# Second graph layer of a fused graph network kernel: weights multiplied first, edge matrix in six blocks, new order at the head

## Chip, cores and metric

The kernel runs on one core of one Trainium2 chip. The metric is the device time of one execution in microseconds, the median of several runs. All times of the trace are counted from the first instruction of the profiled execution.

## What is computed

Two layers on 1250 nodes with 512 features. Each layer adds a graph part and an attention part to x, and then an expert part. The change touches the graph part of the second layer. The reference, cut to it (N = 1250 here, D = 512):

```python
exp_e = jnp.exp(weighting_gate - m)
row_sum = jax.ops.segment_sum(exp_e, src, num_segments=n_nodes)
atten_e = exp_e / (row_sum[src] + 1e-06)
Mfeat = source_features @ Wm + bm                       # 1250 x 256
out0 = jax.ops.segment_sum(atten_e[:, None] * Mfeat[dst], src, num_segments=n_nodes)
out1 = jax.ops.segment_sum(atten_e[:, None] * Mfeat[src], dst, num_segments=n_nodes)
h = jnp.concatenate([out0, out1], axis=-1) @ W1 + b1    # 512 -> 128
h = jax.nn.relu(_layernorm(h, gamma, beta))
h = jax.nn.relu(h @ W2 + b2)                            # 128 -> 512
return jnp.where((row_sum > 0)[:, None], h, 0.0)
```

The sum of this, of x and of the attention part goes through a layer norm, is routed to two banks of eight experts, and the experts' outputs are added.

## The kernel before

Everything runs in one program. Each engine has its own instruction stream, written out by hand, and semaphores order the streams. Nodes are cut into 10 tiles of 125 rows (`NT`, `TP`) and into three column groups of 500, 500 and 250 (`CH`), which hold tiles 0 to 3, 4 to 7 and 8 to 9 (`GROUPS`).

**The order of TensorE's work** is the list `MIX` (line 119 and on). Job j writes bank j mod 8 of PSUM; `begin` (L602) waits until the job eight places earlier has been evacuated; `mx_full` counts finished jobs. VectorE (DVE) and ScalarE (ACT) wait for jobs by name with `mx_wait`.

**Precision.** Ordinary products are split: a float32 operand is stored as a high part and a low part of type float32r, and three products are added (`rows_job`, lines 620 to 622, and `cols_job`, lines 631 to 633). The neighbour sums use plain float32 operands; each of their matmuls stands as two MATMUL records with a weight load each in the trace.

**The edge matrix** (1250 x 1250, the sum of exp(edge weight) over the edges of each pair of nodes) was built at the start and lies in DRAM as `d_w` and transposed as `d_wt`. In the second layer it is read back in slabs of one column group each: `load_slab(i)` (L1234), i = 0 to 2 from `d_wt`, 3 to 5 from `d_w`. There are three homes in SBUF (`slab_home`, L382), so slab i + 3 takes the home of slab i. All six are issued from ACT's DMA queue: 0 after the copies of `bf`, 1 and 2 after the last copy of `x`, 3 to 5 inside the loop at L1320, each after its home's last reader.

**The stretch that is changed, on TensorE:**

- attention jobs `v`, `bq`, `bk`, `source`, `sink` (L816, L826, L832). Between them the features `g`: 10 tiles, xn @ Wm with 256 columns, split precision. ACT copies them to `MfA` (L1254).
- `back`, `bf`, `kv` (L912), `x` (L919) and then `p`, the attention's output projection (10 tiles, 12 matmuls of 512 columns each).
- `rinv` (L930): the inverse row sums turned into rows of 128 equal partitions.
- `ma` and `mb` (L939), 6 jobs each, one for each column group and each half m of the 256 features: 10 matmuls with 128 feature columns as weights and a slab of 500 or 250 columns streamed. DVE scales `ma` by `rinv` into `V` (L1949); ACT and DVE split both into `XH` and `XL`.
- `w1` (`head_in`, L953): 10 tiles, 12 matmuls of 128 columns, the product with W1.
- per group: `head_row` (L1961: add b1, statistics), `spreads` and `scales` (mean, inverse deviation), `head_norm`, ACT's `head_relu` (L1332), `th` (transposes, L964), ACT's `head_cols` (L1337), DVE's `head_low` (L1981), `hd` (`head_out`, L972 to L975: product with W2, four matmuls a tile), ACT's relu (L1359), DVE's `add_row` and statistics of the final layer norm, `norm_rows` (L1111), `store_rows` (L1353), transposes `t7` (L613), `to_cols` (L1084), `low_cols` (L1456), router logits `lg` (L1000 to L1004), `lgt` (L1011).

POOL splits each weight unit into its two parts (L2936, L2938); a unit is 2048 columns. The unit `g1` holds Wm, W1 and W2. The same unit is loaded again as `g1b` for W1 and W2. SP loads the expert weights (`load_bank`, L2851) once the jobs `mb` 5 and `th` 2 are done. ACT's order at the head, as it stands before:

```python
head_cols(0); root(6, 1); head_relu(1); root(6, 2); head_rows(0); head_relu(2)
head_cols(1); head_cols(2); head_rows(1, 2, 3, 4, 5); root(7, 0) ...
```

Of the kernel before, what the change touches and what calls it, by code (L numbers as in the profile page):

```python
# [17 lines left out]
N = 1250  # L18
# [47 lines left out]
COLS = {"bq": 0, "mb1": 4, "fb1": 6, "bs1": 6 + 2 * E0}  # L66
NCOL = 8 + 2 * E0
# [35 lines left out]
def all_of(name, k):  # L103
# [36 lines left out]
       + [("bk", m) for m in range(4)] + [("v", 9), ("shift", 1)]  # L140
# [32 lines left out]
def program(nc, A, out):  # L173
    ctx = ExitStack()
    with ctx:
# [138 lines left out]
        MfA = A3[0:TP, :].rearrange("p (t d) -> p t d", t=NT)  # L314
        MfB = R1[0:TP, 0:NT * 256].rearrange("p (t d) -> p t d", t=NT)
        hg = A3[0:TP, 0:NT * 128].rearrange("p (t d) -> p t d", t=NT)
# [65 lines left out]
        slab_home = [at(AT_Q, NT * 500), A1[:, 0:NT * 500], A2[:, 0:NT * 500]]  # L382

        def slab_of(i):
            return slab_home[i][0:TP, :].rearrange("p (t e) -> p t e", t=NT)
# [49 lines left out]
        slab_loaded = [sem(f"slab_loaded{i}") for i in range(3)]  # L435
# [85 lines left out]
        heavy_rounded = sem("heavy_rounded")  # L521
# [23 lines left out]
        msg_high = sem("msg_high")  # L545
        msg_low = sem("msg_low")
# [28 lines left out]

        def rows_normed(eng, site, t):
            eng.wait_ge(normed_rows, NT * (site - (site > 1)) + t)
# [21 lines left out]
        def stream_pe(pe, n, unit, unit_done):  # L599
# [130 lines left out]
            pe.wait_ge(heavy_ready, 1)  # L730
# [135 lines left out]
            for i in range(3):  # L866
                pe.wait_ge(lo_ready, i + 1)
                for m in range(4):
                    spread_job("bq", 0, 4 * i + m)
                rows_gemm(("v", 6 + i), 6 + i, Hv, Lv, D)  # L870
            for m in range(4):
                spread_job("bk", 1, m)
# [54 lines left out]
            for i, (c0, w) in enumerate(CH):  # L927
                o = begin(("rinv", i))
                for t in range(c0 // TP, (c0 + w) // TP):
                    last = pe.matmul(o[:, TP * t - c0:TP * t - c0 + TP],  # L930
                                     lhsT=rinv[0:TP, t:t + 1].to_broadcast([TP, 128]),
                                     rhs=ident[0:TP, 0:TP], start=True, stop=True, skip_group_check=True)
                last.then_inc(mx_full, 1)

            def message_feature(name, src, i, m):
                c0, w = CH[i]
                o = begin((name, 2 * i + m))[:, 0:w]
                for t in range(NT):
                    last = pe.matmul(o, lhsT=src[:, t, 128 * m:128 * m + 128], rhs=slab_of(i)[:, t, 0:w], start=t == 0,  # L939
                                     stop=t == NT - 1, skip_group_check=True)  # L940
                last.then_inc(mx_full, 1)

            for i in range(3):
                pe.wait_ge(slab_loaded[i], 16)
                pe.wait_ge(features_ready, 1)
                for m in range(2):
                    message_feature("ma", MfA, i, m)
            pe.wait_ge(features_ready, 2)
            Hw, Lw = unit()
            Hw1, Lw1 = (x[:, 1024:1536].rearrange("p (k n) -> p k n", k=KC) for x in (Hw, Lw))  # L950
            Hw2, Lw2 = (x[:, 1536:2048].rearrange("p (k n) -> p k n", k=1) for x in (Hw, Lw))

            def head_in(g):  # L953
                pe.wait_ge(msg_low, 6)
                for m in range(2):
                    mx_evacuated(pe, ("mb", 2 * g + m))
                for t in GROUPS[g]:
                    rows_job(("w1", t), XH, XL, t, Hw1, Lw1, KC, 128)

            def head_turn(g):  # L960
                o = begin(("th", g))
                for t in GROUPS[g]:
                    pe.wait_ge(hg_ready, t + 1 + (g > 1))
# [14 lines left out]
            for i in range(3):  # L978
                pe.wait_ge(slab_loaded[i], 32)
                for m in range(2):  # L980
                    message_feature("mb", MfB, i, m)
                if i:
                    head_in(i - 1)
            head_turn(0)
            head_in(2)
            head_out(0)
            head_turn(1)
            head_turn(2)
            head_out(1)
            turn_group("t7", 7, 0, lambda t: R1t[:, t, :])  # L990
            head_out(2)
            unit_done()

            for g, (c0, w) in enumerate(CH):
                if g < 2:
                    turn_group("t7", 7, g + 1, lambda t: R1t[:, t, :])
# [2245 lines left out]
```

## Time and profile before

| | |
|---|---|
| runs | 1695.72, 1695.84, 1699.32 us; median 1695.84 us |
| span of the profiled execution | 1690.6 us |
| median less span | 5.2 us |
| TensorE busy | 1555.0 us, 92% of the span, 8983 matmul records |
| weight loads busy | 1214.2 us |
| DVE, ACT, POOL busy | 989.6, 445.7, 305.1 us |
| mean granted TensorE clock | 0.972 of full speed |

The execution of the profile has a span, from its first to its last instruction; the time of a run counts some microseconds more around it. A busy TensorE is not a TensorE at its peak, since matmuls are pipelined; the start to start distance of its records tells what one costs.

### The profile page before, as it was taken

To read this page: it belongs to the slowest core of one execution; us is meant where nothing else is said; L and a number is where in the kernel's file an instruction comes from. 1 tells how busy PE (TensorE), PEld (TensorE's weight loads), DVE (VectorE), ACT (ScalarE), POOL (GpSimd) and SP (SyncE) were. 2 spreads that over 40 slices of the span, in tenths; PEclk is the share of its full clock that TensorE was granted. 3 is DMA by queue.
4 is the path that set the end of the run, shared out by engine and by line. 5 is a ranking of instruction groups with operands and counts; after the bars stand their busy time and mean duration, and the time that the engine had idled before them with its cause. 6 is when DMAs were issued, how large, how long until landed. Compare 5 with 4: busy or idle time off the path is not lost.

```text
span 1690.6 us, 23793 instructions
## 1 busy us (share of the span) xinstructions
PE 1555.0 (92%) x8983; PEld 1214.2 (72%) x8983; DVE 989.6 (59%) x1767; ACT 445.7 (26%) x854; POOL 305.1 (18%) x191
## 2 busy tenths in 40 slices
PE   4798988897999999999998999998999999898998
PEld 3686877776777777877786788877757755676765
DVE  7878767889954672397256666665154511763332
ACT  4423111223311220130124242434215101441222
POOL 1000002053111031004001222212211000004565
PEclk9899998999999999999998999999999999899999
DMA  5122324341230020011001010100101322529343
GB/s 158 45 71 91 105 88 164 118 146 52 88 114 27 1 69 25 1 50 68 25 1 51 25 50 26 50 25 26 51 14 53 115 86 80 206 71 316 55 80 44
DMA packets 52138, 123.93 MB, mean 73 GB/s; under 512 B 8417, under 2 KB 28792, under 8 KB 44894
## 3 DMA queue, kind: packets, MB, share of 16 engines
q1 hardware_dynamic: 14026, 65.34, 11.3%
q10 hardware_dynamic: 28147, 46.81, 8.0%
q0 software_dynamic: 9856, 10.28, 3.5%
q8 instruction: 74, 1.21, 0.3%
q14 instruction: 35, 0.29, 0.0%
HBM read 92.87 MB, written 40.22 MB: 79 GB/s over the span
## 4 chain that ended last, share of the span: by engine, by line
PE 75%; DVE 11%; DMA 5%; issue 3%; ACT 3%; POOL 1%; PEld 0%; DVEq 0%; ACTq 0%; PEldq 0%; SPq 0%; POOLq 0%
PE ps L620 9%; PE ps L621 9%; PE ps L622 9%; PE ps L2288 6%; PE ps L678 4%; PE ps L680 4%; PE ps L631 4%; PE ps L632 4%; PE ps L633 4%; PE ps L939 3%; PE ps L3045 3%; PE ps L3067 3%; PE ps L826 2%; DMA d_w<-arena 2%; DMA arena<-d_w 2%
## 5 line engine op out<-in xcount | busy, mean ns | idle before, releaser
L620 PE MATMUL ps<-wslot,XH 128*125 128x512 f32 (+2 forms) x560 | 214.9, 384 | 5.4 <-DVE XL L1456 3.9
L621 PE MATMUL ps<-wslot,XH 128*125 128x512 f32 (+2 forms) x560 | 212.9, 380 | 0.0
L622 PE MATMUL ps<-wslot,XL 128*125 128x512 f32 (+2 forms) x560 | 212.6, 380 | 0.0
L2936 POOL CAST wslot<-arena 128x2048 fp32r<-128x2048 f32 x25 | 47.7, 1908 | 798.3 <-PEq L3013 428.5
L631 PE MATMUL ps<-XH,wslot 128*128 128x500 f32 (+1 forms) x336 | 123.2, 367 | 17.6 <-DVE XL L1456 10.6
L1461 DVE TENSOR_TENSOR arena<-ps,arena 125x512 f32<-125x512 f32 x150 | 98.2, 684 | 51.3 <-PE ps L622 45.3
L620 PEld LDWEIGHTS ps<-wslot,XH 128*125 128x125 f32 x560 | 104.8, 187 | 31.3 <-issue 4.4
L678 PE MATMUL ps<-CTr,Hhi 125*128 125x500 f32 (+1 forms) x360 | 125.0, 361 | 0.0
L632 PE MATMUL ps<-XH,wslot 128*128 128x500 f32 (+1 forms) x336 | 121.8, 362 | 0.0
L633 PE MATMUL ps<-XL,wslot 128*128 128x500 f32 (+1 forms) x336 | 120.9, 360 | 0.0
L622 PEld LDWEIGHTS ps<-wslot,XL 128*125 128x125 f32 x560 | 104.6, 187 | 22.7
L621 PEld LDWEIGHTS ps<-wslot,XH 128*125 128x125 f32 x560 | 104.7, 187 | 21.9 <-issue 0.2
L2288 PE MATMUL ps<-arena 125*128 x1330 | 96.0, 228 | 26.1 <-DVE arena L2562 22.3
L2938 POOL TENSOR_TENSOR wslot<-arena,wslot 128x2048 fp32r<-128x2048 f32 x25 | 117.1, 4685 | 2.0
L680 PE MATMUL ps<-CTr,Hlo_head 125*128 125x500 f32 (+1 forms) x324 | 109.8, 352 | 0.0
L2288 PEld LDWEIGHTS ps<-arena 125*128 125x128 bf16 x1330 | 83.2, 102 | 33.6 <-issue 33.4
L2562 DVE TENSOR_SCALAR arena<-arena 125x1280 bf16<-125x1280 int16 x133 | 73.0, 573 | 43.6 <-PE ps L2288 42.8
L631 PEld LDWEIGHTS ps<-XH,wslot 128*128 128x128 f32 x336 | 65.6, 195 | 31.9 <-issue 18.7
L939 PE MATMUL ps<-arena 125*128 125x500 f32 (+1 forms) x240 | 84.6, 513 | 1.4 <-DMA arena<-d_w 1.4
L1510 DVE TENSOR_TENSOR V<-ps,BC 128x500 f32<-128x500 f32 (+1 forms) x36 | 21.3, 592 | 107.3 <-PE ps L684 106.6
L678 PEld LDWEIGHTS ps<-CTr,Hhi 125*128 125x128 f32 x360 | 67.8, 188 | 15.1 <-issue 5.6
L1129 ACT ACTIVATE V<-V,cols 128x500 f32<-128x500 f32 (+1 forms) x96 | 56.0, 631 | 85.1 <-DVE V L1764 85.1
(445 smaller groups left out, 3074.7 us busy)
## 6 DMA issues: line engine op xcount, KB each, us to landing
arena<-in_units SPq DMA_DIRECT2D x29, 1024.0 KB, 4.8
arena<-in_units SPq DMA_DIRECT2D x8, 2048.0 KB, 11.8
d_w<-arena ACTq DMA_DIRECT2D x10, 625.0 KB
d_wt<-arena ACTq DMA_DIRECT2D x10, 625.0 KB, 4.1
rows<-in_rows ACTq DMA_DIRECT2D x22, 256.0 KB, 4.0
d_kv<-V SPq DMA_DIRECT2D x20, 250.0 KB
arena<-d_kv SPq DMA_DIRECT2D x20, 250.0 KB
arena<-d_wt ACTq DMA_DIRECT2D x2, 2441.4 KB
```

The source lines that it names most:

```text
L620: pe.matmul(o, lhsT=xh[:, k, s], rhs=H4[:, k, 0:nw], start=k == 0, stop=False, skip_group_check=True)
L621: pe.matmul(o, lhsT=xh[:, k, s], rhs=L4[:, k, 0:nw], start=False, stop=False, skip_group_check=True)
L622: last = pe.matmul(o, lhsT=xl[:, k, s], rhs=H4[:, k, 0:nw], start=False, stop=k == K - 1, skip_group_check=True)
L631: pe.matmul(o, lhsT=H4[:, k, f], rhs=XH[:, k, c0:c0 + w], start=k == 0, stop=False, skip_group_check=True)
L632: pe.matmul(o, lhsT=L4[:, k, f], rhs=XH[:, k, c0:c0 + w], start=False, stop=False, skip_group_check=True)
L633: last = pe.matmul(o, lhsT=H4[:, k, f], rhs=XL[:, k, c0:c0 + w], start=False, stop=k == KC - 1, skip_group_check=True)
L678: pe.matmul(o, lhsT=Hhi[0:TP, t, f], rhs=CTr[0:TP, t, c0:c0 + w], start=t == 0, stop=False, skip_group_check=True)
L680: pe.matmul(o, lhsT=Hlo[t][0:TP, f], rhs=CTr[0:TP, t, c0:c0 + w], start=False, stop=False, skip_group_check=True)
L939: last = pe.matmul(o, lhsT=src[:, t, 128 * m:128 * m + 128], rhs=slab_of(i)[:, t, 0:w], start=t == 0, stop=t == NT - 1, skip_group_check=True)
L1461: dve.tensor_tensor(dst, o[0:TP, 0:D], other, ALU.add).then_inc(mx_sem(name), 1)
L2288: last = pe.matmul(ps[:, 3 * (b % 2) + t // 4, 128 * (t % 4):128 * (t % 4) + 128], lhsT=buffer[:, 128 * t:128 * t + 128], rhs=pre_flat[:, ...
L2938: pool.tensor_tensor(wL[unit_slot(u)], wraw, wH[unit_slot(u)].bitcast(F32), ALU.subtract).then_inc(w_ready, 1)
```

## The change

1. The program computes Wm @ W1 on the chip. The unit `g1` now holds Wm transposed. Two new jobs `gw` (12 matmuls each, 256 columns, split precision) give a 512 x 256 matrix, one half for each half of W1; `gb` (4 float32 matmuls, 256 columns) gives bm @ W1. They stand between `v` 8 and `bk` 0. ACT copies them to SBUF, POOL splits the product into high and low part over the place of Wm in `g1`'s slot, and TensorE waits for that (`gw_step` 3) before the jobs `g`. The jobs `g` keep their shape and now give the features times W1, 2 x 128 columns (`GF`).
2. The jobs `rinv`, `ma`, `mb` and `w1` go. In their place are ten jobs `m`, one a tile: 20 float32 matmuls with 125 columns of a slab as weights and 128 columns of `GF` streamed. All copies, scalings and splits of the messages go; DVE's `head_row` scales the first half by `rinv` and adds the other and b1.
3. Each of the six slabs has a home of its own, each is loaded in two DMAs (partitions 0 to 111 and 112 to 124), the three of `d_w` from SP's queue and the three of `d_wt` from ACT's. Waits: after `bf`, after `kv`, after the last `x` (two), after the last `p` (two).
4. The head runs in a new order, and SP's bank loads wait for `m` 7 and `m` 9 instead. `hg` lies in `V`. Some semaphores are split or joined (`heavy_ready`, `hg_normed`, `hd_ready`, `norm_turn`). POOL's routing constants no longer wait for `ma`.

```diff
+       + all_of("gw", 2) + [("gb", 0)] + [("bk", m) for m in range(4)] + [("v", 9), ("shift", 1)]
...
-       + [("x", i) for i in range(12)] + [("p", t) for t in range(10)] + [("rinv", i) for i in range(3)]
-       + all_of("ma", 6) + all_of("mb", 4) + by_tile("w1")[0] + [("mb", 4), ("mb", 5)] + by_tile("w1")[1] + [("th", 0)]
-       + by_tile("w1")[2] + by_tile("hd")[0] + [("th", 1), ("th", 2)] + by_tile("hd")[1]
-       + turned("t7")[0] + by_tile("hd")[2] + turned("t7")[1] + [("lg", 0)] + turned("t7")[2] + [("lg", 1), ("lg", 2)]
+       + [("x", i) for i in range(12)] + [("p", t) for t in range(10)] + all_of("m", 8) + [("th", 0), ("m", 8)]
+       + by_tile("hd")[0] + [("th", 1), ("m", 9)] + by_tile("hd")[1] + turned("t7")[0] + [("th", 2), ("lg", 0)]
+       + by_tile("hd")[2] + turned("t7")[1] + [("lg", 1)] + turned("t7")[2] + [("lg", 2)]
...
+        slab_at = [(AT_Q, AT_R1), (AT_AR, AT_AR + NT * D), (AT_XX, AT_XX + NT * 250)]
...
+        def load_slab(eng, g, half):
+            c0, w = CH[g]
+            for a, b in ROW_PARTS:
+                eng.dma_start(slab_of(g, half)[a:b, :, :],
+                              d_wt[0:N, c0:c0 + w].rearrange("(t p) e -> p t e", p=TP)[a:b, :, :] if half == 0
+                              else d_w[:, a:b, c0:c0 + w].rearrange("t p e -> p t e"))\
+                   .then_inc(slab_loaded[g], 16)
...
+            pe.wait_ge(w_ready, n.unit + 2)
...
+            for i in range(2):
+                o = begin(("gw", i))
+                for c in range(2):
+                    oc = o[:, 256 * c:256 * c + 256].rearrange("p (s n) -> p s n", s=2)
+                    f = slice(256 * i + 128 * c, 256 * i + 128 * c + 128)
+                    for k in range(2):
+                        pe.matmul(oc, lhsT=Ht[:, k, f], rhs=Hw1[:, k, :, :], start=k == 0, stop=False, skip_group_check=True)
+                        pe.matmul(oc, lhsT=Ht[:, k, f], rhs=Lw1[:, k, :, :], start=False, stop=False, skip_group_check=True)
+                        last = pe.matmul(oc, lhsT=Lt[:, k, f], rhs=Hw1[:, k, :, :], start=False, stop=k == 1,
...
+            pe.wait_ge(gw_step, 3)
...
+            def message_rows(t):
+                g = min(t // 4, 2)
+                s = slice(TP * t - CH[g][0], TP * t - CH[g][0] + TP)
+                pe.wait_ge(slab_loaded[g], 64)
+                o = begin(("m", t))
+                for half, feature in enumerate((GA, GB)):
+                    for k in range(NT):
+                        last = pe.matmul(o[0:TP, 128 * half:128 * half + 128], lhsT=slab_of(g, half)[:, k, s],
+                                         rhs=feature[:, k, :], start=k == 0, stop=k == NT - 1, skip_group_check=True)
...
+            head_turn(0)
+            message_rows(8)
+            head_out(0)
+            head_turn(1)
+            message_rows(9)
+            head_out(1)
+            turn_group("t7", 7, 0, lambda t: R1t[:, t, :])
+            head_turn(2)
+            router(0)
+            head_out(2)
+            unit_done()
+            turn_group("t7", 7, 1, lambda t: R1t[:, t, :])
+            router(1)
+            turn_group("t7", 7, 2, lambda t: R1t[:, t, :])
+            router(2)
...
 # ACT
-            for t in range(3, NT):
+            for t in range(3, 9):
                 copy_v(t)
+            for i in range(2):
+                o = mx_wait(act, ("gw", i))
+                act.activation(gw_raw[:, 512 * i:512 * i + 512], o, ACT.Copy).then_inc(mx_sem(("gw", i)), 1)
...
-            load_slab(0)
+            load_slab(act, 0, 0)
...
+            load_slab(act, 1, 0)
+            mx_wait(act, ("p", NT - 1))
+            load_slab(act, 2, 0)
...
+            root(6, 1)
             head_cols(0)
             head_relu(1)
+            head_rows(0, 1, 2, 3)
+            head_cols(1)
+            root(7, 0)
+            norm_rows(7, 0)
+            store_rows(0)
             root(6, 2)
+            head_rows(4, 5)
             head_relu(2)
+            head_rows(6, 7)
+            to_cols("t7", GROUPS[0])
             head_cols(2)
             root(7, 1)
...
 # DVE
             def head_row(t):
+                o = mx_wait(dve, ("m", t))
+                own(dve.scalar_tensor_tensor(hg[:, t, :], o[0:TP, 0:128], rinv[0:TP, t:t + 1], row("gnnA", 128, 256), ALU.mult,
+                                             ALU.add))
+                settle()
+                dve.tensor_tensor(hg[:, t, :], o[0:TP, 128:256], hg[:, t, :], ALU.add).then_inc(mx_sem(("m", t)), 1)
...
+            head_row(8)
+            for t in range(3):
+                head_sum(t)
+            head_low(1)
+            head_sum(3)
+            spreads(0)
+            scales(7, 0)
+            head_row(9)
             spreads(2)
+            head_sum(4)
             scales(6, 2)
             head_norm(2)
+            for t in (5, 6, 7):
+                head_sum(t)
+            spreads(1)
+            low_cols(6, "t7", GROUPS[0])
+            head_low(2)
+            scales(7, 1)
...
 # SP and POOL
-            sp.wait_ge(mx_full, MJ[("mb", 5)] + 1)
+            sp.wait_ge(mx_full, MJ[("kv", 0)] + 1)
+            load_slab(sp, 0, 1)
+            mx_evacuated(sp, ("x", 11))
+            load_slab(sp, 1, 1)
+            sp.wait_ge(mx_full, MJ[("p", NT - 1)] + 1)
+            load_slab(sp, 2, 1)
+            sp.wait_ge(mx_full, MJ[("m", 7)] + 1)
             load_bank(0, 0)
             load_bank(0, 2)
-            sp.wait_ge(mx_full, MJ[("th", 2)] + 1)
+            sp.wait_ge(mx_full, MJ[("m", 9)] + 1)
             load_bank(0, 4)
...
+                if u == UNITS.index("g1"):
+                    pool.wait_ge(gw_step, 1)
+                    pool.tensor_copy(wH[unit_slot(u)][:, 0:1024], gw_raw).then_inc(gw_step, 1)
+                    pool.wait_ge(gw_step, 2)
+                    pool.tensor_tensor(wL[unit_slot(u)][:, 0:1024], gw_raw, wH[unit_slot(u)][:, 0:1024].bitcast(F32),
+                                       ALU.subtract).then_inc(gw_step, 1)
```

## Rows read from the trace of the kernel before

**Rows 1.** The page: span and busy time, share of each engine.
```profile
span 1690.6 us, 23793 instructions
PE 1555.0 (92%) x8983; PEld 1214.2 (72%) x8983; DVE 989.6 (59%) x1767; ACT 445.7 (26%) x854; POOL 305.1 (18%) x191
```

**Rows 2.** The chain that ended last, message stage: start, length, what.
```profile
1349.98 2.49 PE ps L930 x20
1352.47 33.55 PE ps L939 x80
...
1386.76 25.83 DMA arena<-d_w
```

**Rows 3.** Timeline of TensorE: start, length, line, operation, count, idle before.
```profile
1352.30 58.90 PE L939 MATMUL ps<-arena 125*128 125x500 f32 x160
1412.63 17.03 PE L939 MATMUL ps<-arena 125*128 125x500 f32 x40 [1.43 <-DMA arena<-d_w]
...
1448.38 0.61 PE L964 MATMUL ps<-ident,arena 125*128 125x125 f32 x4
...
1492.84 1.26 PE L1011 MATMUL ps<-ident,BC 16*125 16x16 f32 x10
```

**Rows 4.** Windows: stretch, length, busy PE, PEld, DVE, ACT, POOL, clock, DMA.
```profile
1434.70:1443.20 8.50, 8.50 (x40) 7.46 (x40) 1.00 0.00 0
...
1429.10:1434.70 5.60, 5.60 (x51) 5.37 (x49) 2.40 (x7) 1.87 (x2) 0.00 (x0) 1.00 0.00 0
...
1451.40:1492.80 41.40, 33.75 (x124) 18.92 (x123) 30.43 (x87) 23.44 (x44) 0.00 (x0) 0.79 0.58 208
```

**Rows 5.** L912's own records (min/median/max ns); windows of L912 and L3045, columns as rows 4.
```profile
L912 PEld LDWEIGHTS ps<-arena x80: 192/192/333, 1302.6 to 1312.1; 125*128 125x128 f32 x80
L912 PE MATMUL ps<-arena x80: 274/275/421, 1302.8 to 1312.2; 125*128 125x128 f32 x80
...
1302.80:1304.00 1.20, 1.18 (x6) 1.20 (x7) 0.50 0.89 370
...
1543.90:1545.70 1.80, 1.78 (x16) 1.59 (x15) 1.00 1.00 412
```

**Rows 6.** Windows of the feature jobs g 0 to 3 and 4 to 9; columns as rows 4.
```profile
1269.30:1275.20 5.90, 5.90 (x50) 5.77 (x50) 0.08 (x1) 1.62 (x4) 0.00 (x0) 1.00 0.01 3
...
1284.10:1292.90 8.80, 8.69 (x73) 8.49 (x73) 0.41 (x1) 2.50 (x7) 0.00 (x0) 1.00 0.00 0
```

**Rows 7.** Timeline of POOL, the splitting of g1 and of the unit behind it.
```profile
1211.03 4.63 POOL L2938 TENSOR_TENSOR wslot<-arena,wslot 128x2048 fp32r<-128x2048 f32 x1
1258.40 1.89 POOL L2936 CAST wslot<-arena 128x2048 fp32r<-128x2048 f32 x1 [42.74 <-PEq L3013]
```

**Rows 8.** Windows with slab loads, then with stores in two parts; columns as in rows 4.
```profile
1310.00:1320.00 10.00, 9.16 (x39) 5.44 (x38) 6.05 (x10) 2.93 (x5) 0.00 (x0) 1.00 0.33 128
...
1470.50:1479.00 8.50, 4.72 (x23) 3.34 (x23) 5.57 (x17) 4.34 (x9) 0.00 (x0) 0.90 0.76 247
```

**Rows 9.** Timeline of TensorE: tiles hd 1 and hd 2. Then ACT: norm of two rows.
```profile
1452.73 0.50 PE L972 MATMUL ps<-wslot,HH 128*125 128x512 f32 x1
...
1454.05 0.49 PE L972 MATMUL ps<-wslot,HH 128*125 128x512 f32 x1
...
1477.56 1.52 ACT L1111 ACTIVATE arena<-arena,small 125x512 f32<-125x512 f32 x2 [3.23 <-DVEq L1445]
```

**Rows 10.** Timeline of DVE: a norm pair, an add with its statistics, four low parts.
```profile
1438.46 0.35 DVE L1448 SCALAR_TENSOR_TENSOR arena<-arena,small,rows 125x128 f32<-125x128 f32 x1
...
1439.11 0.35 DVE L1448 SCALAR_TENSOR_TENSOR arena<-arena,small,rows 125x128 f32<-125x128 f32 x1
...
1460.44 0.69 DVE L1461 TENSOR_TENSOR arena<-ps,arena 125x512 f32<-125x512 f32 x1
1461.16 0.69 DVE L1419 BATCH_NORM_STATS2 small<-arena 125x6 f32<-125x512 f32 x1
...
1474.16 2.43 DVE L1456 TENSOR_TENSOR XL<-ps,XH 128x500 fp32r<-128x500 f32 x4
```

More of the change, by code:

```diff
@@ L432, in program @@
         ktot = V[0:TP, 0, :]
-        slab_loaded = [sem(f"slab_loaded{i}") for i in range(3)]
+        slab_loaded = [sem(f"slab_loaded{g}") for g in range(3)]
+        gw_step = sem("gw_step")
+        hg_normed = sem("hg_normed")
+        hd_ready = sem("hd_ready")
         ew_turned = sem("ew_turned")
@@ L870, in stream_pe @@
                 rows_gemm(("v", 6 + i), 6 + i, Hv, Lv, D)
+            pe.wait_ge(w_ready, n.unit + 2)
+            after = unit_slot(n.unit + 1)
+            H_, L_ = wH[after], wL[after]
+            Ht, Lt = (w[:, 0:1024].rearrange("p (k n) -> p k n", k=2) for w in (H_, L_))
+            Hw1, Lw1 = (w[:, 1024:1536].rearrange("p (s k n) -> p k s n", s=2, k=2) for w in (H_, L_))
+            for i in range(2):
[7 more added lines that the diff above has]
+                        last = pe.matmul(oc, lhsT=Lt[:, k, f], rhs=Hw1[:, k, :, :], start=False, stop=k == 1,
+                                         skip_group_check=True)
+                last.then_inc(mx_full, 1)
+            o = begin(("gb", 0))[0:TP, 0:256].rearrange("p (s n) -> p s n", s=2)
+            for k in range(2):
+                for part, w1 in enumerate((Hw1, Lw1)):
+                    last = pe.matmul(o, lhsT=cols[:, COLS["bm"] + k:COLS["bm"] + k + 1].to_broadcast([128, TP]),
+                                     rhs=w1[:, k, :, :].bitcast(F32), start=k == 0 and part == 0, stop=k == 1 and part == 1,
+                                     skip_group_check=True)
+            last.then_inc(mx_full, 1)
             for m in range(4):
@@ L926, in stream_pe @@
             unit_done()
[L927 to L932, printed above, removed]
-                last.then_inc(mx_full, 1)
[L935 to L947, printed above, removed]
+            def message_rows(t):
[7 more added lines that the diff above has]
+                                         rhs=feature[:, k, :], start=k == 0, stop=k == NT - 1, skip_group_check=True)
+                last.then_inc(mx_full, 1)
             pe.wait_ge(features_ready, 2)
+            for t in range(8):
+                message_rows(t)
             Hw, Lw = unit()
-            Hw1, Lw1 = (x[:, 1024:1536].rearrange("p (k n) -> p k n", k=KC) for x in (Hw, Lw))
             Hw2, Lw2 = (x[:, 1536:2048].rearrange("p (k n) -> p k n", k=1) for x in (Hw, Lw))
[L953 to L958, printed above, removed]
             def head_turn(g):
@@ L976, in head_out, with router @@
                               skip_group_check=True).then_inc(mx_full, 1)
[L978 to L996, printed above, removed]
+            def router(g):
+                c0, w = CH[g]
                 group_in_cols("t7", g)
@@ L1337, in head_cols @@
                 act.activation(HH[:, 0, c0:c0 + w], o[:, 0:w], ACT.Copy).then_inc(hg_high, 1)
[L1339 to L1340 removed]
             root(6, 0)
             head_relu(0)
[L1343 to L1344 removed]
+            row_ready(act, "gnnb2")
+            act.activation(HH[0:64, 1, 0:D], row("gnnb2")[0:64, :], ACT.Copy).then_inc(hg_high, 1)
             act.wait_ge(w_ready, len(UNITS))
             act.dma_start(b2e, A["b2e"]).then_inc(b2e_loaded, 16)
[L1347 to L1348 removed]
             def store_rows(g):
@@ L1386, in stream_act @@
             store_rows(2)
-            for g, (c0, w) in enumerate(CH):
-                o = mx_wait(act, ("lg", g))
-                act.activation(logits_R[:, c0:c0 + w], o[0:E1, 0:w], ACT.Copy).then_inc(mx_sem(("lg", g)), 1)
-                if g == 0:
-                    to_cols("t7", GROUPS[2])
-            rows_normed(act, 6, NT)
+            router_out(1)
+            to_cols("t7", GROUPS[2])
+            router_out(2)
+            act.wait_ge(hg_normed, NT)
             act.dma_start(b1e, A["b1e"]).then_inc(b1_loaded, 16)
@@ L1982, in head_low, with head_sum @@
                                   ALU.subtract).then_inc(mx_sem(("th", g)), 1)
-            for i in range(4):
-                message_low_b(i)
+            def head_sum(t):
+                dve.wait_ge(hd_ready, t + 1)
+                add_row(("hd", t), R2t[:, t, :], R2t[:, t, :])
+                mx_evacuated(dve, ("hd", t))
+                stats(R2t[:, t, :], t)
             for t in GROUPS[0]:
@@ L2947, in _ @@
                             .then_inc(heavy_scattered, 16)
-            for i in range(6):
-                mx_evacuated(pool, ("ma", i))
             pool.wait_ge(w_ready, len(UNITS))
```

159 lines of the change are left out of this document (45 added, 114 removed).

## Prediction, written before the changed kernel ran

> **What bounds the kernel now.** The page says it first: TensorE is busy 92% of the span [rows 1]. The second view is the chain that ended last. Through the messages it is TensorE's line L939 and, in one place, the slab loads [rows 2]. So a shorter list of matmuls here shortens the kernel, as long as nothing else comes late. The third view is TensorE's timeline from the end of `p` to the start of `lgt`: 1349.98 to 1492.84, 142.9 us [rows 2, 3]. The change replaces nearly all of that stretch, and leaves what follows `lgt` alone. The windows divide the stretch in two. Up to 1451.4 TensorE hardly stops and has full clock. From 1451.4 to 1492.8 it is busy 33.75 of 41.4 us at a mean clock of 0.79, and DVE is busy 30.43 us: there the DVE and ACT norm steps set the pace [rows 4].
>
> The profiled execution has a span of 1690.6 us; the median of the runs is 5.2 us above. I work on the span and add 5.2.
>
> **Removed.** `rinv`: 1349.98 to 1352.30, 2.3 us [rows 2, 3]. `ma` and `mb`: 1352.30 to 1429.10, 76.8 us, which includes the wait of 1.43 us for a slab [rows 3], and 8.5 us for the last column group [rows 4], 85.3 us. `w1` of the first four tiles: 5.6 us [rows 4]. The second four and `th` 0, and the last two, lie between 1443.2, 1448.38 and 1451.4: 5.2 and 3.0 us [rows 3, 4]. Sum 101.4 us; with the 41.4 us of the head that is the 142.8 us again.
>
> **Added on TensorE: the jobs `m`.** 10 tiles x 20 matmuls x 2 records = 400 records of 128 streamed columns, each with its own weight load. This is the biggest term, and it isn't in the trace, but its shape is: L912 (`kv`) has the same form, 125 partitions, 128 weight columns, 128 streamed. Its 80 records start between 1302.8 and 1312.2, 119 ns apart, but the first 1.2 us of it had the half clock, 1.2 GHz [rows 5]. At full clock, L3045 puts 16 records of 128x128 float32 into 1.79 us, 112 ns apart [rows 5]. In the last column group, 40 records of 250 columns took 8.5 us, 212 ns each [rows 4]: so 128 columns alone would be 109 ns, and the weight load costs next to nothing above it. I take 112 ns: 44.8 us, 4.48 a tile; the bounds are 109 (43.6 us) and 119 (47.6 us).
>
> A page speaks against this. The Trainium skill, "TensorE: Matmul & The Clock Gate", section "Part 3: Packing small matmuls", says that a weight load overlaps with running matmuls only where it goes to another row group, and its section "LDWEIGHTS" gives a load as columns over 1.2 GHz, by which 128 columns would be about 107 ns on top of each record's 109: 86 us for the ten tiles, an estimate by those pages. Then the whole gain on the sums would be gone. L912's spacing of 119 ns for load and matmul together speaks against that here.
>
> **Added: `gw` and `gb`.** `gw` is 24 float32r records of 256 columns; `g` ran 72 such in 8.8 us, 122 ns each [rows 6]: 2.9 us. `gb` is 4 float32 matmuls, 8 records of 256 columns, 218 ns each by the 212 ns above: 1.7 us. Together 4.7 us, put where TensorE has no gap: all of it counts. Its waits: `g1`'s parts were ready at 1215.7 [rows 7], long before `v`'s unit is given back at 1258.4 [rows 7], and `gw` stands just ahead of that point, so no wait. Behind it ACT copies two banks, and POOL splits 1024 columns, half of its 1.89 and 4.63 us [rows 7]: 3.3 us. The jobs `g` begin at 1269.3 [rows 6], 11 us after that point, so `gw_step` 3 costs nothing. If that cover went, it would be at most the 3.3 + 1.3 us. POOL is held until about 1263 instead of 1258.4 before it splits the unit of `p` [rows 7], needed at 1326. ACT's `v` 9 copy is queued behind; nobody needs it for 40 us. The jobs in between have three more banks in the ring ahead; each is evacuated within a microsecond.
>
> **Slabs.** Six slabs are 12.5 MB. A slab load on 125 partitions moves 128 GB/s with the DMA share at 0.33 [rows 8]; the one at 1386.76 landed 25.8 us later [rows 2]. The stores of 112 and 13 partitions move 247 GB/s at 0.76 [rows 8], and loads of 128 partitions 412 GB/s at 1.00 [rows 5]. I take 247 for the new loads: 51 us in all. Issues begin at 1303 + 4.7 = 1308 and the first four slabs (10 MB) are needed at 1354.7 and, for tiles 4 to 7, at 1372.6; the last two at 1391. At 247 GB/s four slabs take 40 us. Two of them start only after the last `x`, at 1331, and these 5 MB land by about 1352. No wait, so the 1.43 us go too. ACT's splits of `x` are now behind two issues instead of one, in a gap of 11 us: nothing.
>
> **The head.** I lay its order out with the durations of before, counted from the end of `p`. TensorE: `hd` 1.32 us a tile [rows 9], `th` 0.6 for four, `t7` 0.66 a tile, `lg` 2.7 us for a group of 500 and 1.4 for 250. DVE: add with statistics 1.32 a tile, a norm pair 0.65, four low parts 2.4 [rows 10], `spreads` 0.7, `scales` 0.8 to 1.0, and the new `head_row` 1.0, an estimate: a two-operation step with its wait, one add, statistics, each about a third of a microsecond. ACT: relu of a tile 0.6, norm of a row 0.76 [rows 9], a store with two issues 1.0, `to_cols` 0.5 a tile.
> `m` 7 ends at 35.8. `th` 0 and `m` 8 hide the first group's transposes and low part, to 40.9. `hd` 0 to 3, `th` 1, `m` 9, `hd` 4 to 7 and four `t7` follow without a gap, to 59.2. Here TensorE stops. DVE has worked through rows 7 and 8, the second norms, four adds, then row 9 to 52.9. It waits 3.4 us for ACT (four norm rows, store, root, relu). Then come one add, two norms, three adds, `spreads` and the low parts: 67.1. TensorE gets `th` 2 in between at 60.6. It idles 1.4 + 6.3 us. `lg` 0 and `hd` 8, 9: 72.5. ACT and DVE need up to 80.6 for the next group, another 5.5 us of idle. `lg` 1, two `t7`, `lg` 2: 87.3. `lgt` starts at 88.1. So the head after the ten tiles costs 43.3 us against 41.4.
> The same durations laid over the order of before, from 1429.1, put `lgt` 65.7 us later; the trace has 63.7 [rows 3, 4]. The list is 2 us long. I keep it, since the new gaps of 6 us are longer, and the matmuls behind gaps ran in part at half clock before (mean 0.79) [rows 4]; both ends, -2 and +4, go to the range.
>
> **Sum.** 88.1 + 4.7 = 92.8 against 142.9: 50.1 us less. Span 1640.5, time 1645.7 us. POOL's constants (2.4 us at 1395) move under `m`, the bank loads keep their distance to `lgt` (36 and 52 us before it), and the last waits for `hd` 9 as before: zero.
>
> **The rivals.**
> (a) *Slab loads no faster than before.* If two parts move 125 GB/s as one did, 10 MB from 1308 on are there at 1388, 15.4 us after tile 4 wants them, and 12.5 MB at 1408, 17.3 us after tile 8: 1663. For it: packets are as short as before. Against: the stores in two parts. 8%.
> (b) *Slower: the same place, worse.* Now two queues load at once, beside TensorE reading slabs. The mean rate decides. Below 94 GB/s the 12.5 MB take 133 us, 50 us more than the 83 between 1308 and 1391, and the whole gain is eaten; at 85 GB/s it would be 64 us, 1710. For it: only that no row shows two slab loads in flight on two queues. Against: one queue alone moved 128 GB/s [rows 8] on what the share of 0.33 shows to be a third of the engines. 2%.
> (c) *Weight loads don't hide.* Each record pays its load. 109 + 107 by the page; from rows alone, the recorded load and matmul end to end (192 + 275 ns [rows 5]) are the far bound, 187 us, slower by 92. By the milder form 86 us for the tiles, 1687. For it: 400 alternating pairs, twenty to a bank. Against: 119 and 112 ns in this trace for the same shape. 4% for the mild form, under 1% for the far one.
> (d) *The head is DVE's.* The tail loses more than the list says: every longer gap is followed by half clock, and `head_row` costs 1.5 instead of 1.0. `lg` and `hd` at half clock add 6 us, the rows 2 where DVE is late: 1654. For it: DVE is nearly without a pause from 36 to 67. 14%.
> (e) *The program does less than it says*, for instance waits for `gw` because POOL is late: at most 4.6 us, 1650; inside the range.
>
> **How the numbers follow.** Forecast 1646, 71%, with its own range 1640 to 1655. The range reaches from 1639 (109 ns, list 2 us long, -1 for a gap) up to 1661, which takes in (d) and (e) and part of (a); above it lie most of (a), then (b), (c). A measurement of this kernel tells about 0.2%, 3.4 us, from no change. Faster by more than that: all of the forecast, (a), (d), (e) and the mild (c), 0.96. Within 0.2%: 0.015. Slower: 0.025, from (b) and the far (c).
>
> **What would show it.** In the trace of after: 400 records of 128 columns that start 112 ns apart, at full clock, 44 to 45 us from first to last tile without the pieces between; no wait for a DMA before a tile; `gw` and `gb` together 4.7 us; no wait for POOL before `g`; two gaps of TensorE of 5 to 7 us, before `lg` 0 and `lg` 1, both ended by DVE's low parts; `lgt` about 88 us after the last `p`. Wrong it would be if the tiles were 8 us each (c), if tile 4 or 8 waited for its slab (a, b), or if something after `lgt` that I leave alone came late: the expert banks or the stored rows.

## The result, and the profile after

The changed kernel takes 1646.17 us (median, 1641.70 to 1648.24) against 1697.58 (1695.72 to 1699.64) for the kernel before in the same comparison: ratio 0.9697, 95% interval 0.9675 to 0.9719. The forecast was 1646.

The page of the changed kernel, span and engines (against [rows 1]): 52 more matmul records, and 51.7 us less busy time on TensorE.

```profile
span 1645.9 us, 23879 instructions
PE 1503.3 (91%) x9035; PEld 1200.8 (73%) x9035; DVE 985.0 (60%) x1759; ACT 439.5 (27%) x842; POOL 307.0 (19%) x193
```

TensorE's timeline of the changed kernel, from `gw` to `lgt` (start, length, line, operation, count, idle before it and what ended that). It answers [rows 2, 3].

```profile
1257.48 0.28 PE L896 MATMUL ps<-wslot 128*128 128x256 f32 x1
...
1260.34 1.89 PE L904 MATMUL ps<-wslot,cols 128*125 128x256 f32 x8
...
1308.03 1.63 PE L846 MATMUL ps<-HH,HL 104*128 104x500 f32 x8 [0.57 <-DVE HH L1895]
...
1356.25 35.17 PE L972 MATMUL ps<-arena 125*125 125x128 f32 x320 [0.26 <-issue]
...
1391.68 4.53 PE L972 MATMUL ps<-arena 125*125 125x128 f32 x40
...
1401.68 4.53 PE L972 MATMUL ps<-arena 125*125 125x128 f32 x40
...
1422.23 0.58 PE L1005 MATMUL ps<-XH,wgH 128*16 128x500 f32 x1 [6.47 <-DVE XL L1462]
...
1438.16 0.58 PE L1005 MATMUL ps<-XH,wgH 128*16 128x500 f32 x1 [6.18 <-DVE XL L1462]
...
1446.23 1.26 PE L1032 MATMUL ps<-ident,BC 16*125 16x16 f32 x10
```

The tiles `m` (L972) run without a wait. Two gaps remain, one ahead of each of the first two routers (L1005), both ended by DVE's low parts (L1462). The records of `m` (min/median/max ns, first and last start), then the chain that ended last at the first gap (start, length, what):

```profile
L972 PEld LDWEIGHTS ps<-arena x400: 184/188/189, 1356.2 to 1405.8; 125*125 125x125 f32 x134
L972 PE MATMUL ps<-arena x400: 272/273/346, 1356.2 to 1405.9; 125*125 125x128 f32 x134
```

```profile
1418.22 0.70 DVE small L1425
1418.95 0.39 DVE small L1431 x4
1419.65 2.35 DVE XL L1462 x4
1421.99 0.24 issue
1422.23 0.58 PE ps L1005
```

Windows of the changed kernel (columns as [rows 4]; where four numbers follow the length they are PE, clock, DMA share, GB/s): the first eight tiles, the slab loads (the first of these windows also holds the load of a weight unit), the first gap, router 0, and the stretch behind `lgt`.

```profile
1356.25:1391.30 35.05, 35.05 (x321) 35.05 (x322) 11.47 (x40) 3.71 (x7) 8.75 (x13) 1.00 0.33 79
...
1308.00:1318.00 10.00, 9.97 (x84) 1.00 0.97 278
1318.00:1328.00 10.00, 9.16 (x31) 1.00 1.06 191
...
1338.00:1348.00 10.00, 10.00 (x45) 1.00 1.05 288
...
1413.20:1422.20 9.00, 0.62 (x2) 0.28 (x2) 8.57 (x22) 4.43 (x10) 0.00 (x0) 0.71 0.33 126
1422.20:1427.20 5.00, 4.96 (x13) 1.91 (x14) 0.84 (x6) 1.52 (x2) 0.00 (x0) 0.50 0.00 0
...
1446.20:1453.00 6.80, 6.80 (x36) 5.82 (x36) 4.58 (x14) 5.09 (x7) 0.00 (x0) 1.00 0.02 5
```

Where the 44.7 us between the two profiled spans lie (read from the timelines of both; "start of m" is in the kernel before the start of `rinv`, both follow the last `p`):

| stretch | before | after | difference |
|---|---|---|---|
| start to one product group of `bq` (L832, now L846) | 1243.64 | 1246.75 | +3.1 |
| from there to the start of m | 106.34 | 109.50 | +3.2 |
| start of m to `lgt` | 142.86 | 89.98 | -52.9 |
| `lgt` to the end of the span | 197.8 | 199.7 | +1.9 |

The third line is the change, the second is `gw` and `gb`. The first and the last are stretches that the change leaves alone; they are followed up below.

### The profile page after: what moved, and what is told of

The parts are those of the page before. It is cut to its first block, busy times and chain, and to the rows that moved or that the text cites. A ratio compares the mean times of both kernels' runs of the same rounds, so it can differ in the third digit from the quotient of the medians.

```text
span 1645.9 us, 23879 instructions
## 1 busy us (share of the span) xinstructions
PE 1503.3 (91%) x9035; PEld 1200.8 (73%) x9035; DVE 985.0 (60%) x1759; ACT 439.5 (27%) x842; POOL 307.0 (19%) x193
## 4 chain that ended last, share of the span: by engine, by line
PE 76%; DVE 12%; issue 4%; DMA 3%; ACT 3%; POOL 1%; PEld 0%; DVEq 0%; ACTq 0%; PEldq 0%; POOLq 0%
PE ps L634 9%; PE ps L635 9%; PE ps L636 9%; PE ps L2273 6%; PE ps L692 5%; PE ps L694 4%; PE ps L645 4%; PE ps L646 4%; PE ps L647 4%; PE ps L3040 3%; PE ps L3062 2%; PE ps L972 2%; PE ps L840 2%; DMA d_w<-arena 2%; PE ps L2188 1%
## 5 line engine op out<-in xcount | busy, mean ns | idle before, releaser
L634 PE MATMUL ps<-wslot,XH 128*125 128x512 f32 (+1 forms) x520 | 204.4, 393 | 5.6 <-DVE XL L1462 3.9
L635 PE MATMUL ps<-wslot,XH 128*125 128x512 f32 (+1 forms) x520 | 202.6, 390 | 0.0
L636 PE MATMUL ps<-wslot,XL 128*125 128x512 f32 (+1 forms) x520 | 202.1, 389 | 0.0
L634 PEld LDWEIGHTS ps<-wslot,XH 128*125 128x125 f32 x520 | 97.5, 187 | 31.3 <-DVE XL L1462 4.3
L636 PEld LDWEIGHTS ps<-wslot,XL 128*125 128x125 f32 x520 | 97.5, 188 | 23.0
L635 PEld LDWEIGHTS ps<-wslot,XH 128*125 128x125 f32 x520 | 97.6, 188 | 21.8
L1516 DVE TENSOR_TENSOR V<-ps,BC 128x500 f32<-128x500 f32 (+1 forms) x36 | 21.3, 592 | 107.3 <-PE ps L698 106.5
L634 PE MATMUL ps<-wslot,HH 128*125 128x512 f32 x180 | 72.8, 404 | 3.4 <-DVE HL L1759 3.4
## 6 DMA issues: line engine op xcount, KB each, us to landing
arena<-in_units SPq DMA_DIRECT2D x8, 2048.0 KB, 10.8
```

Of the source, the lines that this page charges most:

```text
L634: pe.matmul(o, lhsT=xh[:, k, s], rhs=H4[:, k, 0:nw], start=k == 0, stop=False, skip_group_check=True)
L635: pe.matmul(o, lhsT=xh[:, k, s], rhs=L4[:, k, 0:nw], start=False, stop=False, skip_group_check=True)
L636: last = pe.matmul(o, lhsT=xl[:, k, s], rhs=H4[:, k, 0:nw], start=False, stop=k == K - 1, skip_group_check=True)
```

## The experiments

All are set beside the kernel before on their own chip. The changed kernel itself, once more:

> The changed kernel once more, unchanged, as the measure for the other runs of this chip: 1646 us. Its profile had the first 1243 us of work, which the change doesn't touch, 3.1 us later than the profile of before. If that is chance, the same work here starts somewhere else, earlier or later by a few us; if the change causes it, it is again some 3 us late.

Measured: 1648.6 us, ratio 0.9715 (0.9692 to 0.9738); the `bq` group starts at 1247.87, late again, `m` at 1357.38, `lgt` 91.2 us later, and the span ends at 1647.2.

**Slabs in one part.** Each slab load as one DMA of 125 partitions, as the kernel before has it (the count that TensorE waits for is halved to match):

```
-                for a, b in ROW_PARTS:
+                for a, b in ((0, TP),):
                     eng.dma_start(slab_of(...)[a:b, ...], ...)
```

> Only edit: each slab is loaded in one DMA of 125 partitions instead of two of 112 and 13; homes, queues and times of issue stay. My theory: the two parts are what makes the loads quick. One part moves about 125 GB/s, also when both queues load; 10 MB issued from 1310 on are there at 1390, tile 4 wants them at 1374: a wait of 16 us before tile 4 and some 2 us before tile 8, 1646 + 17 = 1663 us. Rival: the homes and early issues alone are enough, or two queues double the rate (250 GB/s): no wait, 1646 us.

Measured: 1674.5 us, ratio 0.9878 (0.9857 to 0.9899), 26 us above the changed kernel. Its timeline, then one window (length, PE, clock, DMA share, GB/s):

```profile
1363.97 20.08 PE L972 MATMUL ps<-arena 125*125 125x128 f32 x160 [7.73 <-DMA arena<-d_w]
1399.04 19.64 PE L972 MATMUL ps<-arena 125*125 125x128 f32 x160 [14.99 <-DMA arena<-d_wt]
```

```profile
1350.00:1370.00 20.00, 12.27 (x60) 0.74 0.33 125
```

So rival (a) was a real danger, and the row parts are what averts it. With loads under way on both queues the share stays at 0.33 and the rate at 125 GB/s, what one queue alone had in [rows 8]; in 112 and 13 partitions the share is about 1.0 and the rate 191 to 288 GB/s. The waits are 22.7 us together, not the 17.3 of rival (a): I had the slabs arrive one after the other, but two queues shared the rate, so that even the first tile waited 7.7 us. Another 4.6 us are lost behind the waits: the eight tiles take 20.08 + 19.64 us in place of 35.17, as the clock is at 0.50 for the first 3.5 to 4 us behind each wait.

The Trainium skill, "DMA: Bandwidth & Descriptors", section "Why a DMA increments its semaphore by 16 and not by 1", says that a transfer is spread over the largest number of engines up to 16 that divides its slowest dimension, starting from the lowest-numbered one. Worked out from that rule, an estimate, 125 gives 5 of 16 and 112 gives 16. The share of 0.33 agrees, and so does it that a second queue adds nothing if it uses the same five.

**The same in the kernel before.** Its slab loads in two parts:

> The kernel before with one part of the change alone: each slab load in two DMAs of 112 and 13 partitions, homes and issue points as before. The loads get quick, but only one wait of 1.4 us hung on them: 1.4 us less, 1694.5 us, no difference that can be measured. Rival: quick loads at full share disturb the matmuls beside them, or the added issues hold ACT: a few us slower.

Measured: 1696.5 us, ratio 0.9999 (0.998 to 1.0017), and no wait for a slab is left. There the one wait of 1.4 us was all that the loads cost, and its loss doesn't show: from `rinv` to `lgt` it is 144.8 us, against 142.9 and 144.0 in the two profiles of the kernel before. No run takes the six homes or the second queue away from the changed kernel, so what these two are worth is not shown.

**The old order at the head.** `hd`, `th`, `t7` and `lg` in the order of before on TensorE, ACT and DVE, behind ten unbroken tiles of `m` (TensorE's part of the edit, its lines joined):

```
-            head_turn(0); message_rows(8); head_out(0); head_turn(1); message_rows(9); head_out(1)
+            message_rows(8); message_rows(9); head_turn(0); head_out(0); head_turn(1); head_turn(2); head_out(1)
```

> Only edit: the head's order is that of the kernel before on TensorE, ACT and DVE; all ten tiles m come first. The list of durations by which I predicted puts the router's end (start of lgt) 91.3 us after the last p instead of 88.0: 3 us slower, 1649 us, since the tiles 8 and 9 no longer cover the first groups' transposes. Rival: the order is the greater part of what the head costs, 8 us or more slower, since the gaps bring the half clock; or it is worth nothing because DVE has the same work.

Measured: 1647.6 us, ratio 0.9719 (0.9691 to 0.9746). Its timeline:

```profile
1357.13 43.90 PE L972 MATMUL ps<-arena 125*125 125x128 f32 x400 [0.26 <-issue]
...
1430.94 3.66 PE L627 MATMUL ps<-ident,arena 125*128 125x125 f32 x16 [3.64 <-ACT arena L1132]
...
1446.99 1.26 PE L1032 MATMUL ps<-ident,BC 16*125 16x16 f32 x10
```

89.9 us from the start of m to `lgt`, as with the new order (90.0 and 91.2). The new order is worth nothing. It hides `th` and the first low parts behind two tiles of `m`, but TensorE's waits from there to `lgt` are 16.6 us long in all, mostly in two pieces, against 10.8 us in five pieces here. The old order loses as much by slower work: the second `t7` group takes 3.66 us against 1.90 in the changed kernel, and from 1411 to 1420 the clock is at 0.50. The 400 records give the cleanest price: 43.90 us, 110 ns each.

**Half the sum.** Each tile's products run over 5 of the 10 row blocks (it leaves out half of the neighbour sum):

```
-                    for k in range(NT):
+                    for k in range(5):
```

> Leaves out half of the neighbour sum: 5 instead of 10 matmuls for each half of each tile m, 200 records fewer; its output is not the reference's. If a record costs 112 ns of the path, TensorE has 22.4 us less. The tiles 8 and 9 are then too short to cover the transposes, and the list of durations keeps 16.6 us of it: about 1629 us. If the weight loads were hidden less well than I took it, more than 22.4 us would go from the ten tiles; if the head were DVE's altogether, the eight tiles ahead of it would still give 18 us.

Measured: 1629.6 us, ratio 0.9611 (0.9587 to 0.9634). Its timeline:

```profile
1355.76 17.70 PE L972 MATMUL ps<-arena 125*125 125x128 f32 x160 [0.26 <-issue]
1373.72 2.35 PE L972 MATMUL ps<-arena 125*125 125x128 f32 x20
1383.38 2.35 PE L972 MATMUL ps<-arena 125*125 125x128 f32 x20
1430.07 1.26 PE L1032 MATMUL ps<-ident,BC 16*125 16x16 f32 x10
```

200 records fewer are 21.8 us fewer on TensorE; `lgt` comes 15.7 us sooner (74.3 us after the start). So through the tiles TensorE sets the pace, but not for the whole of the saving: its waits for DVE and ACT grow from 16.6 to 21.4 us.

**Without the folded weights.** `gw`, `gb` and POOL's step for them are left out, so the feature weights are not those of the reference:

> The changed kernel without gw and gb, without their copies and POOL's split (its features are then not multiplied by W1, so its output is not the reference's). My theory: they lie bare on TensorE's path, 4.4 us in the profile: 1646 - 4.4 = 1642 us. Rival: two short waits behind them (0.6 and 0.8 us, before bf and before x) come back as DVE or ACT ends last there, and only 3 us are won.

Measured: 1646.5 us, ratio 0.9708 (0.9687 to 0.9729). From the `bq` group to the start of m 106.5 us against 109.5: `gw` and `gb` cost 3.0 us, though they take 4.4 (1257.48 to 1261.88). The median is no help here: its ratio is no lower than that of the changed kernel (0.9697 and 0.9715). The rest of the 4.4 us comes back at one place. The eight products that follow DVE's wait at the end of the attention stage, in this kernel, as the timeline and a window show them:

```profile
1303.11 2.66 PE L846 MATMUL ps<-HH,HL 104*128 104x500 f32 x8 [0.59 <-DVE HH L1863]
```

```profile
1303.10:1307.00 3.90, 3.89 (x16) 0.56 0.80 276
```

2.66 us at a mean clock of 0.56, where the changed kernel has 1.63 (above) at 1.00. In each of the five profiles without `gw` (the kernel before twice, its two variants, and this kernel) the same eight records took 2.16 to 2.75 us; in each of the nine with it, 1.62 to 1.65. Up to this wait TensorE has the full clock with and without `gw`. So the steps that `no_gw` leaves out (4.4 us on TensorE, more than 40 us upstream, with ACT's copies and POOL's split) decide whether TensorE is at 1.2 or 2.4 GHz here; which of them, and by what path, is open.

**Tiles 8 and 9 ahead of the router.** TensorE runs `hd` 8 and 9 before router 0, and ACT and DVE take their steps in that order:

```
             head_turn(2)
-            router(0)
             head_out(2)
             unit_done()
+            router(0)
```

> A new order of the head: hd 8 and 9 before the router of group 0; on ACT the relu of hd 4 and the root of the last rows before the four norm rows, the stores later, hd 8 and 9 before the second norm rows; on DVE the last low part and scales before the four low parts. By the list of durations lgt starts 82.8 instead of 88.0 us after the last p, 5 us earlier: 1641 us. If the tail is a matter of which DVE and ACT step comes first this shows; if the half clock behind TensorE's gaps eats it, it is 1644 or no change.

Measured: 1645.9 us, ratio 0.9702 (0.968 to 0.9725). Its timeline:

```profile
1423.12 0.79 PE L994 MATMUL ps<-wslot,HH 128*125 128x512 f32 x1 [6.10 <-DVE HL L1963]
...
1427.81 0.38 PE L1005 MATMUL ps<-XH,wgH 128*16 128x500 f32 x1 [0.36 <-issue]
...
1436.03 0.39 PE L1005 MATMUL ps<-XH,wgH 128*16 128x500 f32 x1 [3.62 <-DVE XL L1461]
...
1444.37 1.26 PE L1032 MATMUL ps<-ident,BC 16*125 16x16 f32 x10
```

The second gap shrinks from 6.2 to 3.6 us, and `lgt` follows the start of m (1359.93) by 84.4 us, 5.5 less than 90.0. The median hardly shows it (0.9702 against 0.9697 and 0.9715), since the time ahead of m varies too: this profiled execution started m 3.7 us later than that of the changed kernel. What moves that start is the next question.

**Is it the layout?** All profiles of the changed kernel up to here had been 2.7 us or more late at `bq`. The texts below call that group the last `bq` product; it is the first of the three. Two variants exchange the layouts: the changed kernel with the two new columns behind all other tensors (`slim`), and the kernel before with two unused columns.

```
-        cols = sb("cols", [128, NCOL])
+        cols = sb("cols", [128, NCOL - 2])        # slim; cols_bm = sb("cols_bm", [128, 2]) behind iota8
```

> The changed kernel with the bias's two columns in a tensor of their own behind all others, so that every other tensor of the main layout stands where the kernel before has it. If the 3 us by which all profiles of the changed kernel are behind at the last bq product (1246.3 to 1250.4 against 1243.1 to 1245.5) come from addresses that shifted by 8 bytes a partition, this one has it at about 1243.5 and runs 3 us faster, ratio 0.970. If they come from chance or from the size of the program, it is at 1247 and the ratio 0.972.

> The kernel before with two unused columns more in cols, the layout of the changed kernel. By the addresses: last bq product at about 1246.5 and a time 3 us above the kernel before, ratio 1.002. By chance or the program's size: 1243 to 1245 and ratio 1.000.

Measured: `slim` 1651.8 us, ratio 0.9726 (0.9704 to 0.9748), `bq` at 1253.98 and m at 1363.48, the latest of all; the padded kernel before 1698.9 us, ratio 1.0008 (0.9994 to 1.0022), `bq` at 1247.20. The padded kernel alone would fit the addresses. But `slim` has the old addresses and is 10 us late, and `filler` below, with the layout of the changed kernel, has `bq` at 1242.55, the earliest of all. So the addresses don't explain the 3 us. The kernel before, once more:

> The kernel before, unchanged, for a second profile: 1696 us. In five profiles of the changed kernel and its variants the last job bq starts between 1246.3 and 1247.9 us; in the one profile of before it was 1243.6. If the change has nothing to do with it, this profile has it near 1247 too.

Measured: 1696.8 us, ratio 1.001 (0.9996 to 1.0025), `bq` at 1243.09. The first stretch varies from one profiled kernel to the next by up to 11 us (start of m 1352.1 to 1363.5 among kernels that differ only behind it or in two columns). Nearly all of it arises in the first 440 us: one split of POOL's starts at 430.48 in `filler` and at 441.98 in `slim`, 11.5 us apart, and at `bq` they are 11.4 us apart. What varies there is open. Two profiles that agree, here 1243.64 and 1243.09, were no proof of anything.

**Keeping TensorE at work in its gaps.** Products that nobody reads, into the router's own bank before it is filled, 24 ahead of router 0 and 20 ahead of router 1:

```
+                for _ in range(24 if g == 0 else 20):
+                    pe.matmul(o[0:16, 0:500], lhsT=HH[:, 0, 0:16], rhs=HH[:, 0, 0:500], start=True, stop=True, ...)
                 group_in_cols("t7", g)
```

> The changed kernel, with products that nobody reads put into two waits of TensorE: 24 of 500 columns (0.23 us apart at the full clock, 5.5 us) while it waits 6.5 us ahead of the first router, 20 (4.6 us) in the 6.2 us ahead of the second. If the idle stretch is what lets the granted clock fall, both routers run at the full clock: the first takes 2.7 us in place of 5.0, the second 2.7 in place of 4.0, and from the end of p to lgt 90.0 us becomes about 86.5 (the second router's wait for VectorE may swallow the first's gain: then 88.7). If the clock falls for another reason (the engines beside it, or too few rows at work), the window stays near 0.56 to 0.59, the products themselves run slow (24 x 0.41 = 10 us), the first router starts 3 us later and the stretch becomes 93.

Measured: 1648.8 us, ratio 0.9712 (0.9691 to 0.9733). Its timeline, then windows of router 0 and of the stretch behind `lgt`:

```profile
1411.42 7.12 PE L1002 MATMUL ps<-HH 128*16 128x500 f32 x24
1418.38 0.39 PE L1013 MATMUL ps<-XH,wgH 128*16 128x500 f32 x1
...
1425.61 4.66 PE L1002 MATMUL ps<-HH 128*16 128x500 f32 x20
...
1438.78 1.94 PE L1040 MATMUL ps<-ident,BC 16*125 16x16 f32 x10
```

```profile
1418.40:1421.10 2.70, 2.70 (x13) 1.22 (x12) 0.50 (x4) 1.52 (x2) 0.00 (x0) 1.00 0.00 0
...
1438.80:1445.60 6.80, 6.80 (x23) 5.83 (x23) 4.10 (x13) 3.79 (x5) 0.00 (x0) 0.53 0.01 2
```

Router 0 runs at the full clock, 2.7 us in place of 5.0, and so does router 1 (2.7 in place of 4.0). The 24 products themselves took 7.1 us and not 5.5, at a mean clock of 0.76. `lgt` comes 86.7 us after the start of m (1352.09), 3.3 less than 90.0. But the time gains nothing: behind `lgt` the clock is 0.53 where the changed kernel has 1.00, 23 records fit where 36 did, and `lgt` to the end takes 203.7 us instead of 199.7. So in this profile the gain was given back behind `lgt`, most of it in this first stretch (6.8 us at 0.53 are 3.2 us lost).

**Order and fillers together.** The order of `hd_first`, 24 such products ahead of tile 8 and 14 ahead of router 1, and the columns placed as in `slim`:

> The order of hd_first (84.4 us from the end of p to lgt), with such products in the 6.1 us ahead of the head's tile 8 (24 of them) and in the 3.6 us ahead of the second router (14), and the columns of the bias in a tensor of their own at the end of the layout. By the clock theory tiles 8 and 9 take 3.3 us in place of 4.7 and the first router stays at 2.7: 83 us. Against the kernel before: p to lgt about 60 us less, ratio 0.967 to 0.970; without any gain from the clock it is hd_first again, 0.970.

Measured: 1639.9 us (1639.37 to 1644.72), ratio 0.966 (0.964 to 0.9679). Its timeline and the window behind `lgt`:

```profile
1417.66 5.56 PE L1007 MATMUL ps<-HH 128*16 128x500 f32 x24
1423.97 0.49 PE L999 MATMUL ps<-wslot,HH 128*125 128x512 f32 x1 [0.75 <-DVE HL L1976]
...
1442.20 1.26 PE L1045 MATMUL ps<-ident,BC 16*125 16x16 f32 x10
```

```profile
1442.20:1449.00 6.80, 6.80 (x36) 5.87 (x36) 4.61 (x14) 5.10 (x7) 0.00 (x0) 1.00 0.01 5
```

81.4 us from the start of m (1360.84) to `lgt`, against 83 forecast, and 1.00 behind it. This is the fastest version. Its interval ends below the starts of those of `hd_first` (0.968, by a hair), of the changed kernel's repeat (0.9692) and of `filler` (0.9691); only `filler` and `slim` were measured on the same chip. With the first measurement of the changed kernel (0.9675 to 0.9719) it just overlaps.

The stretches from the start of m (of `rinv` before), which leave the first stretch's spread out:

| kernel | m to `lgt` | `lgt` to end | m to end |
|---|---|---|---|
| before | 142.9 | 197.8 | 340.6 |
| before, repeated | 144.0 | 197.6 | 341.6 |
| before, two parts | 144.8 | 198.9 | 343.7 |
| before, padded | 144.4 | 199.4 | 343.8 |
| after | 90.0 | 199.7 | 289.7 |
| after, repeated | 91.2 | 198.6 | 289.8 |
| `old_order` | 89.9 | 198.4 | 288.3 |
| `no_gw` | 90.8 | 198.4 | 289.2 |
| `slim` | 91.0 | 198.0 | 288.9 |
| `filler` | 86.7 | 203.7 | 290.4 |
| `hd_first` | 84.4 | 198.9 | 283.4 |
| `best` | 81.4 | 200.6 | 282.0 |

## Why the prediction was right, point by point

**The bound.** TensorE's list set the stretch, and a shorter list shortened it by 52.9 us against 54.8 forecast. That the list is what counts is shown by `half_k`, and where it stops counting too.

**The tiles `m`.** 110 ns a record against 112, 44.2 us of busy time against 44.8. The last column group of [rows 4], 212 ns for 250 columns, was the better row: its half, and next to nothing for the load. `ma` and `mb` streamed 100,000 columns in 85.3 us, `m` streams 51,200 in 44.2. In the window of the first eight tiles PEld is busy all of 35.05 us beside PE, so the loads are hidden and rival (c) is refuted. (The prediction says that by the page's rule the whole gain would be gone. Its own sum for (c), 1687 us, would have left 9 us of it.) The rule of "Part 3: Packing small matmuls" doesn't hold for this stream. The same page of the Trainium skill, "TensorE: Matmul & The Clock Gate", says in "Step-by-step: what each phase is for" that a load may also go to a background weight buffer while a matmul runs; 110 ns a record agree with that.

**`gw` and `gb`.** 4.4 us against 4.7, all of which I counted. The step that was off is "all of it counts": only 3.0 to 3.2 did, since the half clock at the end of the attention stage disappeared. The waits were as forecast: POOL splits the part by 1264.4, and no job `g` waits.

**The slabs.** No wait, as forecast, at 191 to 288 GB/s where 247 was taken. `one_part` shows that the gain was at risk here, and that (a), had it come, costs 26 us and not 17. Two queues with parts did not run at (b)'s low rates.

**The head.** Counted from the start of m: tile 7 ends at 35.0 (35.8 forecast), the first `t7` group at 56.9 (59.2), router 0 starts at 66.0 (67.1), router 1 at 81.9 (80.6), `lgt` at 90.0 (88.1). At router 0 the list was 1.1 us long; laid over the order of before it had been 2 us long. Router 0 then took 5.0 us instead of 2.7, at a clock of 0.50 behind a gap of 6.5, and router 1 took 4.0. These 3.6 us are the piece of rival (d) that came true; its 6 us were too much here, as `hd` 8 and 9 had the full clock again. The end I had kept (-2 and +4) held it. In the last steps the recorded sum has a gap: from 80.6 on, `lg` 1, two `t7` and `lg` 2 add up to 86.0, not 87.3. The 1.3 us more stand for no named term, and the trace has a wait of 1.62 us there, ahead of `lg` 2.

**The sum.** 92.8 us forecast for `gw`, `gb` and m to `lgt`, 93.1 measured (3.16 + 89.98): this agrees well, with +1.9 on the head against -1.5 on `gw` and `gb`. The span was 1645.9 against 1640.5: the other 5 us are +3.1 ahead of the change and +1.9 behind it. And the 5.2 us that I set between span and median were two things. In every recorded run of the kernel before 1.7 to 1.8 us lie outside the span, and in those of the changed kernel 1.7 to 3.1 us (1647.91 against 1645.9 in the profiled one). The other 3.5 us of the 5.2 would mean that the profiled execution of before was a quick one; its own time is not on record. The median of after came out at 1646.17. The medians differ by 51.4 us, the stretch from `bq` to `lgt` by 49.7; 50.1 were forecast. So the closeness to 1646 is partly luck: the untouched stretches alone scatter by more than the difference.

**What was not foreseen at all** is that the new order is worth nothing here (`old_order`), and that one exchange in it (`hd_first`) would have been worth 5.5 us of the stretch from m to `lgt`.

## What to carry to other kernels

Where a chain of matmuls by the same small matrix ends a stage, multiply the weights first and stream the narrow result: the time fell with the streamed columns, and 128-column float32 records hid their weight loads. Before you count on such a gain, look at what feeds the shorter list: here the transfers had to run at twice the rate, and did not do so with 125 partitions in one DMA, even on two queues. Compare stretches that start at the change; an untouched stretch ahead of it scattered by up to 11 us, and would have hidden a gain of 5.

## What the runs showed of the hardware

- Two queues with 125-partition loads move 125 GB/s together, as one does (share 0.33). In 112 and 13 partitions the share is about 1.0 and the rate 191 to 288 GB/s.
- The granted clock can depend on what was done far upstream. Eight records at the end of the attention stage take 2.2 to 2.75 us without `gw` more than 40 us earlier and 1.62 to 1.65 with it, in 14 profiles without an exception. The cause is not settled.
- Filling TensorE's gaps keeps the clock of the next products at 2.4 GHz (router 0: 5.0 to 2.7 us), but it can fall in the next stage instead, in the middle of a stretch in which TensorE is busy (0.53 for 6.8 us behind `lgt` in `filler`). With other gaps (`best`) it didn't. A filler is worth its stretch only if the stages behind it keep their clock too; one profile each shows this, and what decides it is open.
- A float32 product is two records, each at 110 ns for 128 streamed columns and 212 for 250, weight load included.
